# A mixture-of-experts layer in two waves: batches split five to three, denser dispatch in attention, a shorter gather at the end

## The chip, the cores and the metric

The kernel runs on one core of one Trainium2 chip. The metric is the device time of one execution in microseconds. The program is written by hand for the engines: PE (TensorE, matrix products), ACT (ScalarE), DVE (VectorE), POOL (GpSimd) and SP (SyncE, which here only issues DMA transfers). Each engine works through its own list of instructions in order; they meet only in semaphores.

## The reference

Input x is 8 batches of 512 tokens of 256 float32 values. What is computed:

```
q = elu(x@Wq+bq)+1;  k = elu(x@Wk+bk)+1;  v = x@Wv+bv        # 16 heads of 16
kv   = einsum('bhsd,bhse->bhde', k, v)                        # per batch
attn = einsum('bhsd,bhde->bhse', q, kv)
x = layernorm(x + (sigmoid(x@Wg+bg) * attn) @ Wo + bo)
# routing: softmax over 16 experts in 4 groups, the best 2 groups, the best 4 experts in them
y = sum over the 4 chosen experts e of  c[t,e] * (silu(x@w1[e]) * (x@w3[e])) @ w2[e]
z = (silu(x@ws1) * (x@ws3)) @ ws2                             # shared expert
x = layernorm(x + y + z)
```

There are 4096 tokens and so 16384 pairs of token and expert. Experts have an inner width of 128, the shared one of 256.

## The kernel before

**Layout.** Batch b has 4 tiles of 128 tokens; tile k is tile k % 4 of batch k // 4. All activations stay on the chip in `x_all`.

**Attention and routing (to about 270 us).** PE, DVE and POOL have `batch` (PE from L1228, DVE from L902) written out eight times. For batch b the engines project, sum k and v, attend to batch b, and finish batch b-1: residual and layer norm (DVE `bn_stats` L691 and `bn_aggr` L699, then POOL `rstd_of` L424 to L431 with four small operations, then ACT L510), transposes of the result, `route` (PE L1211/L1212, whose products DVE reads at L730) and, for batch b-2, `assign_slots` (DVE L793 to L804), which gives each token its four rows in a table sorted by expert.

**Dispatch.** POOL's `dispatch` (L434 to L441) writes 128 token rows of 1 KB into this table in DRAM (`expert_in`) with one indirect DMA: one per tile and choice, so 16 per batch. The table has a part for each of two waves of four batches, and 64 dispatches fill one. In each of the attention batches b = 3 to 7 POOL has four places for `SPREAD` = 3 of them: after `kv_projected`, after `rstd_of(b-1)` (these two and the third come close together), after `q_projected`, and after `kv_summed`. The last 4 follow. The 64 of wave 1 are sent in sixteen bursts of four while PE works on wave 0, the i-th gated by the pair 5i//2.

**Planning.** When batch 3's slots are known, `count_region` (called in batch 5) tells SP where regions end, and `plan_pairs` cuts the table into pairs of 256 rows: 48 per wave. The instructions L844, L849, L850 and L854 go over 48x16 numbers on one partition.

**Experts.** A pair is one block of 256 rows: SP loads it, PE transposes (L1340), multiplies up (L1149 to L1151) and down (L1367), ACT does silu (L634) and copies, DVE the product (L1036) and the low parts (L1025, L1044), SP stores the result into `expert_out`. The ring has four places; PE, ACT and SP run in hardware loops, DVE too in most of each wave. The shared expert runs for three batches (`EARLY`) ahead of the pairs and for five after them.

**Gathering.** POOL's `gather` (L443 to L454) fetches, for one tile, four times 128 rows from `expert_out`, into one of four places `y_got`; DVE's `combine` (L1055) adds each, weighted, to `x_all`. All 16 tiles of wave 0 are gathered and combined while the pairs of wave 1 run, at one or two combines per pair, with final norms of batches 0 to 2. The gather of tile k waits for `combined` of tile k-4.

**The end.** After the last store of `expert_out`, POOL gathers wave 1's 16 tiles: four batches of 16 indirect DMAs, with `rstd_of(NB + b - 1)` after the gathers of batch b. Meanwhile PE and ACT do the shared expert of batches 3 to 7, and DVE takes, in a fixed order, `shared_hidden`, 8 of the tiles' combines inside it, `add_shared(n)` (L1002), the final norm (L1070) and the moments (L691, L699); the other 8 tiles come after `add_shared(7)`. SP stores each batch's output of 512 KB when its norm is done.

## Time and profile before

| what | value |
|---|---|
| median of three runs | 701.73 us (698.48 to 703.09) |
| the profiled execution | 698.33 us, its span 696.5 us |
| mean granted clock of TensorE | 0.925 |
| attention and routing | 0 to about 270 us |
| wave 0's pairs | about 270 to 437 us |
| wave 1's pairs, to the last store | about 437 to 590 us |
| gathers of wave 1, remaining sums and norms | 590 to 696.5 us |

The profile is of one execution on the only core. "Idle before" an instruction is given in brackets with what ended it; `remote` or `another core or an unknown queue` stands where the profile finds no releaser in its records (there is no other core at work here). `issue` is time in which an engine waited for nothing that the profile shows. Where ACT or DVE work in a pair, the names of tiles are those of buffers used again (`kv_heads` is silu's result, `q_fm`, `gate` and `wa_stage` hold gathered rows, `gated` the output).

### The profile page before, as it was taken

The numbers are of one execution on the slowest core, as the hardware profiler recorded it, in microseconds if no ns is written. First come the engines' busy times: TensorE is split into PE (matmuls) and PEld (weight loads), VectorE is DVE, ScalarE is ACT, GpSimd is POOL, SyncE is SP. The second block draws the span as 40 slices with busy tenths as digits, with TensorE's granted clock in tenths as the row PEclk, the third lists the DMA queues.
The fourth block names the chain that finished last, engine by engine and source line by source line (L and its number), as shares of the span: only waits on it lengthen the run. The fifth ranks groups of instructions, "written<-read, shape, count | busy, mean of one in ns | idle before, by whom it ended". The sixth has DMA issues, their size and how long they took to land.

```text
span 696.5 us, 13485 instructions
## 1 busy us (share of the span) xinstructions
PE 517.0 (74%) x3554; PEld 355.2 (51%) x3555; DVE 427.1 (61%) x1200; ACT 300.6 (43%) x659; POOL 290.6 (42%) x334
## 2 busy tenths in 40 slices
PE   1899886789897787888886787888887779782300
PEld 1355543455454356676674566676765666441100
DVE  2447783777755877557654344366757657585384
ACT  2536644446334252555554555355645446121000
POOL 1000126365455421545644200634435450787664
PEclk9999999799999989999999999899999999997555
DMA  7022338285561302677767776677777763334232
GB/s 193 25 76 77 124 118 288 75 274 192 202 225 54 113 31 69 220 231 241 252 243 247 252 226 210 189 232 226 222 246 230 240 198 137 99 120 123 83 113 98
DMA packets 64091, 118.63 MB, mean 170 GB/s; under 512 B 9760, under 2 KB 23088, under 8 KB 64048
## 3 DMA queue, kind: packets, MB, share of 16 engines
q1 hardware_dynamic: 51216, 84.55, 37.2%
q0 software_dynamic: 12288, 33.57, 15.4%
q8 instruction: 19, 0.31, 0.2%
q14 instruction: 24, 0.20, 0.1%
q10 hardware_dynamic: 544, 0.00, 0.0%
HBM read 55.17 MB, written 62.91 MB: 170 GB/s over the span
## 4 chain that ended last, share of the span: by engine, by line
PE 35%; issue 17%; DVE 17%; SPq 8%; POOL 7%; ACT 5%; DMA 5%; another core or an unknown queue 5%; DVEq 0%; ACTq 0%; POOLq 0%
PE t L1340 4%; PE h_even L1149 3%; PE h_even L1151 3%; PE h_even L1150 3%; PE h_odd L1149 3%; PE h_odd L1151 3%; PE h_odd L1150 3%; DMA kv<-expert_in 2%; PE y L1186 2%; SPq L327 2%; POOL q_fm L452 2%; SPq L330 2%; POOL wa_stage L452 2%; POOL gate L452 2%
## 5 line engine op out<-in xcount | busy, mean ns | idle before, releaser
L440 POOL DMA_INDIRECT expert_in<-x_all,slots x128 | 132.9, 1038 | 111.7 <-PE h_odd L1151 45.1
L1340 PE MATMUL t<-ident,kv 128*128 128x128 f32 x384 | 61.7, 283 | 23.8 <-DMA kv<-expert_in 16.6
L452 POOL DMA_INDIRECT wa_stage<-expert_out,result_of x64 | 62.9, 982 | 28.2 <-issue 17.5
L452 POOL DMA_INDIRECT q_fm<-expert_out,result_of x32 | 32.1, 1003 | 89.8 <-DMA expert_out<-q_exp 64.1
L1044 DVE TENSOR_TENSOR wa_lo<-bias_heads,wa_hi 128x256 bf16<-128x256 f32 x96 | 40.5, 422 | 46.6 <-ACT wa_hi L642 37.2
L426 POOL TENSOR_SCALAR neg_mean<-mv 128x4 f32<-128x4 f32 x16 | 4.6, 290 | 148.7 <-DVE mv L699 148.5
L1340 PEld LDWEIGHTS t<-ident,kv 128*128 128x128 f32 x384 | 44.9, 145 | 33.8 <-issue 17.6
L1025 DVE TENSOR_TENSOR xsT_lo<-t,xsT_hi 128x512 bf16<-128x512 f32 x72 | 49.4, 688 | 13.2 <-ACT xsT_hi L617 6.6
L1150 PE MATMUL h_even<-xsT_lo,we_hi 128*128 128x256 bf16 x192 | 53.6, 279 | 2.2 <-issue 2.2
L1149 PE MATMUL h_even<-xsT_hi,we_hi 128*128 128x256 f16 x192 | 53.5, 279 | 1.8 <-DVE bias_heads L1036 1.3
L1151 PE MATMUL h_even<-xsT_hi,we_lo 128*128 128x256 f16 x192 | 53.6, 279 | 1.2 <-issue 1.1
L617 ACT ACTIVATE xsT_hi<-t 128x512 f16<-128x512 f32 x72 | 42.1, 587 | 17.9 <-PE t L1340 12.7
L1367 PE MATMUL y<-we_hi,wa_hi 128*128 x96 | 26.9, 281 | 27.8 <-issue 15.5
L642 ACT ACTIVATE wa_hi<-bias_heads 128x256 f16<-128x256 f32 x96 | 39.7, 413 | 16.0 <-DVE bias_heads L1036 10.6
L1186 PE MATMUL y<-wo_sb,gated 128*128 128x256 f32 x128 | 33.5, 421 | 12.0 <-DVE gated L686 12.0
L452 POOL DMA_INDIRECT gate<-expert_out,result_of x32 | 31.2, 976 | 19.7 <-PE h_even L1151 10.8
L1036 DVE TENSOR_TENSOR bias_heads<-h_odd,kv_heads 128x256 f32<-128x256 f32 x48 | 20.1, 420 | 31.4 <-ACT kv_heads L634 31.4
L1036 DVE TENSOR_TENSOR bias_heads<-h_even,kv_heads 128x256 f32<-128x256 f32 x48 | 20.1, 419 | 31.3 <-ACT kv_heads L634 19.2
L624 ACT ACTIVATE q_exp<-y 128x512 f32<-128x512 f32 x48 | 28.6, 597 | 23.4 <-PE y L1373 18.1
L529 ACT ACTIVATE kv<-h_even 128x256 f32<-128x256 f32 x32 | 12.4, 386 | 59.4 <-PE h_even L1151 53.1
L1186 PEld LDWEIGHTS y<-wo_sb,gated 128*128 128x128 f32 x128 | 26.8, 213 | 19.2 <-DVE gated L686 14.7
L634 ACT ACTIVATE kv_heads<-h_odd 128x256 f32<-128x256 f32 x48 | 18.3, 382 | 41.9 <-remote 22.0
(222 smaller groups left out, 1522.0 us busy)
## 6 DMA issues: line engine op xcount, KB each, us to landing
kv<-expert_in SPq DMA_DIRECT2D x96, 256.0 KB
expert_out<-k_exp SPq DMA_DIRECT2D x48, 256.0 KB
expert_out<-q_exp SPq DMA_DIRECT2D x48, 256.0 KB
expert_in<-wa_stage SPq DMA_DIRECT2D x16, 512.0 KB
expert_in<-wa_stage SPq DMA_DIRECT2D x32, 256.0 KB
stage<-in_L_ffn_w SPq DMA_DIRECT2D x48, 128.0 KB
x_in<-in_L_attn_x SPq DMA_DIRECT2D x8, 512.0 KB
out<-gated SPq DMA_DIRECT2D x8, 512.0 KB
```

The source lines that it names most:

```text
L440: pool.indirect_dma_start(xs_dram[b // WB], bass.IndirectOffsetOnAxis(ap=slots[:, b, t, j:j + 1], axis=0), x_all[:, b, t, :], None).then_i ...
L452: pool.indirect_dma_start(y_got[i][:, j, :], None, ys_dram[w], bass.IndirectOffsetOnAxis(ap=result_of[:, b, t, j:j + 1], axis=0)).then_inc ...
L617: act.activation(xsT_hi[r][:, :, :], t_bank[r % 2][:, :].rearrange("p (c n) -> p c n", c=KC), ACT.Copy).then_inc(xst_hi_ready, 1)
L642: act.activation(aT_hi[r % 2][:, :], a_pair, ACT.Copy).then_inc(at_hi_ready, 1)
L1025: dve.tensor_tensor(xsT_lo[r][:, :, :], t_bank[r % 2][:, :].rearrange("p (c n) -> p c n", c=KC), xsT_hi[r][:, :, :], ALU.subtract).then_in ...
L1036: dve.tensor_tensor(a_pair, h_banks[r % 2][0][:, 2 * P:], s_pair, ALU.mult).then_inc(pair_a_ready, 1)
L1044: dve.tensor_tensor(aT_lo[r % 2][:, :], a_pair, aT_hi[r % 2][:, :], ALU.subtract).then_inc(at_lo_ready, 1)
L1149: pe.matmul(dst, sta_hi, mov_hi, start=start, stop=False)
L1150: pe.matmul(dst, sta_hi, mov_lo, start=False, stop=False)
L1151: return pe.matmul(dst, sta_lo, mov_hi, start=False, stop=stop)
L1186: last = pe.matmul(y_bank[h][:, (t % 2) * D:(t % 2 + 1) * D], gated[:, c, t * P:(t + 1) * P], wo_sb[:, c, :], start=c == 0, stop=c == KC - 1)
L1340: last = pe.transpose(t_bank[r % 2][:, c * 2 * P + i * P:c * 2 * P + (i + 1) * P], xs[r][:, i, c * P:(c + 1) * P], ident[:, :])
```

## The change

The waves get five and three batches, so 56 and 40 pairs instead of 48 and 48. In the attention stage all 80 dispatches of wave 0 are sent, 16 in each of the batches 3 to 7 (`SPREAD` 4) and none after; the 48 of wave 1 follow in twelve bursts of four, one every four pairs of wave 0. `count_region(0)` moves from batch 5 to batch 6. The planning operations of both waves are made for up to 56 pairs.

In wave 1, DVE's code is written out pair by pair. It combines 18 of wave 0's 20 tiles (72 combines) evenly over the pairs 6 to 39, and the final norms of batches 0 to 2 lie one tile per pair at pairs 16, 23 and 31. POOL's gathers of these 20 tiles are gated at pair 17k//9 of wave 1.

At the end 12 tiles are gathered instead of 16. Ten tiles (18 to 27) are combined inside the shared expert's steps, four (batch 7) after `add_shared(7)`. The final `rstd` is made of two POOL operations instead of four, and their places between the gathers change. The last batch has moments, `rstd`, norm and output store in two halves; the `rstd` of its first half is asked for ahead of the gather of its last tile.

```diff
-SPREAD = 3
+SPREAD = 4
@@
-    WB = NB // WAVES
-    WT = WB * TT
-    NPAIR = WT * TOP_K // 2 + E
+    BATCHES = (5, 3)
+    START = (0, BATCHES[0], NB)
+    TILES = [TT * n for n in BATCHES]
+    NPAIR = [n * TOP_K // 2 + E for n in TILES]
+    SUM_PAIRS = (6, 40)
+    SUMMED = 18
+    NORM_PAIR = (16, 23, 31)
@@ sync
-            with sp.Fori(WB - 2, NB) as b:
+            with sp.Fori(EARLY - 1, NB - 1) as b:
                 store_out(b)
-            sp.wait_ge(out_stored, 16 * NB)
+            for h in range(2):
+                half = slice(2 * h, 2 * h + 2)
+                sp.wait_ge(out_ready, NB + h)
+                sp.dma_start(out[NB - 1].rearrange("(p t) d -> p t d", p=P)[:, half, :], o_sb[:, half, :]).then_inc(out_stored, 16)
+            sp.wait_ge(out_stored, 16 * (NB + 1))
@@ gpsimd
+            def final_rstd(ln, of=slice(0, TT)):
+                pool.wait_ge(mv_ready, ln + 1)
+                pool.tensor_tensor(var_eps[:, of], mv[:, of, 1], eps[:, of], ALU.add).then_inc(rstd_step, 1)
+                pool.wait_ge(rstd_step, NB + ln + 1)
+                pool.tensor_tensor(rstd[:, of], var_eps[:, of], minus_half[:, of], ALU.pow).then_inc(rstd_ready, 1)
@@ gather(k)
-                if 0 < k < WT:
-                    pool.wait_ge(h_ready, NPAIR + (3 * k if k < WT - TT else 3 * WT - 13 + 2 * (k - WT + TT)))
+                if w == 0 and k > 0:
+                    pool.wait_ge(h_ready, FIRST[1] + 17 * k // 9)
@@
-            for i in range(WT):
+            for i in range(TILES[1]):
                 if i > 0:
-                    pool.wait_ge(h_ready, 5 * i // 2)
+                    pool.wait_ge(h_ready, 4 * i)
                 dispatch(rows[first + TOP_K * i:first + TOP_K * (i + 1)])
@@
                         gather(TT * b + t)
-                        if b > 0 and t == (1 if w == 0 else TT - 1):
-                            rstd_of(NB + b - 1)
-            rstd_of(2 * NB - 1)
+                        if w == 0 and t == TT - 2 and 0 < b <= EARLY:
+                            final_rstd(NB + b - 1)
+                        if b == NB - 1 and t == 1:
+                            final_rstd(2 * NB - 2)
+                        if b == NB - 1 and t == 2:
+                            final_rstd(2 * NB - 1, slice(0, 2))
+                    if w == 1 and b < NB - 1:
+                        for ln in range(EARLY if b == START[1] else b - 1, b):
+                            final_rstd(NB + ln)
+            final_rstd(2 * NB, slice(2, TT))
@@ vector
-            batch(5, True, True, True, early=PAIRS - 1, plan=True)
-            batch(6, True, True, True)
+            batch(5, True, True, True, early=PAIRS - 1)
+            batch(6, True, True, True, plan=True)
@@
-            with dve.Fori(1, EARLY) as b:
-                group(q1 + 1 + 3 * b, b, thirds[0])
-                group(q1 + 2 + 3 * b, b, thirds[1], norm=b - 1)
-                group(q1 + 3 + 3 * b, b, thirds[2])
+            for i in range(SUMMED * TOP_K):
+                at = SUM_PAIRS[0] + i * (SUM_PAIRS[1] - SUM_PAIRS[0]) // (SUMMED * TOP_K)
+                sums[at].append((i // (TT * TOP_K), i // TOP_K % TT, i % TOP_K))
+            for p in range(NPAIR[1]):
+                pair(FIRST[1] + p, p % RING, p < NPAIR[1] - 2, sums[p], norms.get(p))
@@
-            for n in range(WB, NB):
-                at = 2 * (n - WB)
+            for n in range(EARLY, NB):
+                at = SHARED * (n - EARLY)
                 shared_hidden(SHARED * n, tiles[at])
                 shared_hidden(SHARED * n + 1, tiles[at + 1])
@@
-            for b in range(WB + 2, NB):
-                for t in range(TT):
-                    for j in range(TOP_K):
-                        combine(1, b, t, j)
-                    if t == 2:
-                        whole_norm(b - 1)
-            whole_norm(NB - 1)
+            for w, b, t in tiles[SHARED * (NB - EARLY):]:
+                for j in range(TOP_K):
+                    if (t, j) == (1, TOP_K - 1):
+                        whole_norm(b - 1)
+                    combine(w, b, t, j)
+                if t >= 2:
+                    final_norm(b, 2 * t - 4)
+                    final_norm(b, 2 * t - 3)
```

## Rows read from the trace of the kernel before

**Rows 1.** The page: span, busy time and instructions of the engines.
```profile
span 696.5 us, 13485 instructions
PE 517.0 (74%) x3554; PEld 355.2 (51%) x3555; DVE 427.1 (61%) x1200; ACT 300.6 (43%) x659; POOL 290.6 (42%) x334
```

**Rows 2.** The last chain, 100 to 240 us: start, length, what.
```profile
110.49 10.35 another core or an unknown queue
...
145.49 3.38 another core or an unknown queue
...
173.17 3.31 another core or an unknown queue
```

**Rows 3.** Timeline of POOL, dispatches and a wait beside attention: start, us, what [idle before].
```profile
102.87 2.00 POOL L440 DMA_INDIRECT expert_in<-x_all,slots  x1 [0.18 <-issue]
...
118.02 0.96 POOL L440 DMA_INDIRECT expert_in<-x_all,slots  x1 [0.30 <-issue]
...
148.29 0.96 POOL L440 DMA_INDIRECT expert_in<-x_all,slots  x1 [0.30 <-issue]
...
175.98 0.96 POOL L440 DMA_INDIRECT expert_in<-x_all,slots  x1 [0.30 <-issue]
...
187.52 0.23 POOL L426 TENSOR_SCALAR neg_mean<-mv 128x4 f32<-128x4 f32 x1 [5.06 <-DVE mv L699]
```

**Rows 4.** Timeline of DVE, where it takes the router's products, and a planning operation.
```profile
86.61 0.29 DVE L730 TENSOR_REDUCE logits<-t 128x64 f32<-128x128 f32 x1 [0.81 <-PE t L1212]
...
120.85 0.29 DVE L730 TENSOR_REDUCE logits<-t 128x64 f32<-128x128 f32 x1 [10.37 <-remote]
...
227.81 0.29 DVE L730 TENSOR_REDUCE logits<-t 128x64 f32<-128x128 f32 x1 [1.95 <-remote]
...
232.53 0.94 DVE L844 TENSOR_TENSOR stage<-plan_sb,pairs_end 1x768 f32<-1x768 f32 x1
```

**Rows 5.** Timeline of PE: the router's last product of batch 2.
```profile
111.07 0.18 PE L1212 MATMUL t<-gwT_both,xT_lo 128*128 128x32 f16 x1
```

**Rows 6.** Timeline of ACT, one silu per pair: pairs 2, 51, 52, 59, 91, 95.
```profile
277.55 0.38 ACT L634 ACTIVATE kv_heads<-h_even 128x256 f32<-128x256 f32 x1
...
436.83 0.38 ACT L634 ACTIVATE kv_heads<-h_odd 128x256 f32<-128x256 f32 x1 [0.28 <-PE h_odd L1151]
446.22 0.38 ACT L634 ACTIVATE kv_heads<-h_even 128x256 f32<-128x256 f32 x1 [6.58 <-remote]
...
466.06 0.38 ACT L634 ACTIVATE kv_heads<-h_odd 128x256 f32<-128x256 f32 x1 [0.28 <-PE h_odd L1151]
...
574.56 0.38 ACT L634 ACTIVATE kv_heads<-h_odd 128x256 f32<-128x256 f32 x1 [0.94 <-remote]
...
582.81 0.38 ACT L634 ACTIVATE kv_heads<-h_odd 128x256 f32<-128x256 f32 x1 [0.41 <-PE h_odd L1151]
```

**Rows 7.** Timeline of POOL: gathers at the start of wave 1.
```profile
436.18 1.21 POOL L452 DMA_INDIRECT q_fm<-expert_out,result_of  x1 [46.19 <-DMA expert_out<-q_exp]
...
445.20 0.95 POOL L452 DMA_INDIRECT gate<-expert_out,result_of  x1 [0.30 <-issue]
```

**Rows 8.** Timeline of POOL: the end.
```profile
590.97 0.94 POOL L452 DMA_INDIRECT q_fm<-expert_out,result_of  x1 [17.95 <-DMA expert_out<-q_exp]
...
611.80 0.26 POOL L426 TENSOR_SCALAR neg_mean<-mv 128x4 f32<-128x4 f32 x1
...
663.71 1.07 POOL L452 DMA_INDIRECT q_fm<-expert_out,result_of  x1 [4.82 <-DVE x_all L1055]
...
690.12 0.23 POOL L426 TENSOR_SCALAR neg_mean<-mv 128x4 f32<-128x4 f32 x1 [4.34 <-DVE mv L699]
```

**Rows 9.** Timeline of DVE: the end.
```profile
652.84 1.29 DVE L1002 TENSOR_TENSOR x_all<-y,x_all 128x512 f32<-128x512 f32 x2 [7.88 <-remote]
...
680.76 2.05 DVE L1055 SCALAR_TENSOR_TENSOR x_all<-wa_stage,c_of_slot,x_all 128x256 f32<-128x256 f32 x4 [2.57 <-DMA wa_stage<-expert_out,result_of]
...
691.94 1.38 DVE L1070 TENSOR_SCALAR gated<-x_all,mv,rstd 128x256 f32<-128x256 f32 x4 [1.91 <-POOL shift L431]
```

More of the change, by code:

```diff
@@ L353, in _ @@
             sp.wait_ge(rows_ready, 1)
-            for b in range(WB):
+            for b in range(BATCHES[0]):
                 sp.wait_ge(dispatched[b], 16 * TT * TOP_K)
@@ L364, in _ @@
             sp.wait_ge(fill_rows_ready, 2)
-            with sp.Fori(3, (last - 1) // 2) as q2:
+            with sp.Fori(3, 5) as q2:
                 group(0, 2 * q2 + 1, fill=E + 2 * RING * (q2 - 3))
                 group(0, 2 * q2 + 2, fill=E + 2 * RING * (q2 - 3) + RING)
+            for q in range(11, last):
+                group(0, q)
             sp.wait_ge(rows_ready, 2)
-            for b in range(WB, NB):
+            for b in range(BATCHES[0], NB):
                 sp.wait_ge(dispatched[b], 16 * TT * TOP_K)
@@ L693, in norm_stats, with norm_moments @@
                 norm_moments(ln)
-            def norm_moments(ln):
+            def norm_moments(ln, of=slice(0, TT)):
                 dve.wait_ge(bn_ready, ln + 1)
                 dve.memset(wait_pad[:, :], 0.0)
-                for t in range(TT):
+                for t in range(TT)[of]:
                     last = dve.bn_aggr(mv[:, t, :], bn[:, t, :])
@@ L868, in place_results @@
                     tiles = slot_of[:, of_wave, :, :].rearrange("p b t e -> p (b t) e")
-                    dve.tensor_tensor(tiles, tiles, closer[:, w:w + 1, :].to_broadcast([P, WT, E]), ALU.add).then_inc(result_step, 1)
+                    dve.tensor_tensor(tiles, tiles, closer[:, w:w + 1, :].to_broadcast([P, TILES[w], E]), ALU.add).then_inc(result_step, 1)
                 if part in (1, 2):
                     dve.wait_ge(result_step, at + 1)
-                    for b in range(WB * w + 2 * part - 2, WB * w + 2 * part):
+                    middle = START[w] + (BATCHES[w] + 1) // 2
+                    for b in range(*((START[w], middle) if part == 1 else (middle, START[w + 1]))):
                         for t in range(TT):
@@ L939, in batch @@
                 if plan:
-                    count_region(0, WB - 1)
+                    count_region(0, BATCHES[0] - 1)
             xt_lo(0)
@@ L1026, in xst_lo, with pair @@
                                   xsT_hi[r][:, :, :], ALU.subtract).then_inc(xst_lo_ready, 1)
-            def pair(g, r, ahead=True, add=None, norm=None, whole=True, part=None):
+            def pair(g, r, ahead=True, add=(), norm=None, part=None):
                 if ahead:
@@ L1044, in pair, with combine @@
                 dve.tensor_tensor(aT_lo[r % 2][:, :], a_pair, aT_hi[r % 2][:, :], ALU.subtract).then_inc(at_lo_ready, 1)
-                if add and len(add) > 1:
-                    combine(0, *add[1], whole)
-            def combine(w, b, t, j, whole=True):
+                for some in add[1:]:
+                    combine(0, *some)
+            def combine(w, b, t, j):
                 if j == 0:
                     dve.wait_ge(y_gathered[t], 16 * TOP_K * (b + 1))
-                if late(b, 1) or t > 0 or j > 0:
+                if b > 0 or t > 0 or j > 0:
                     dve.wait_ge(combined, TOP_K * (TT * b + t) + j)
@@ L1060, in combine @@
                     last = dve.bn_stats(bn[:, t, :], x_all[:, b, t, :])
-                    if t == TT - 1:
+                    if b == NB - 1 and t % 2 == 1:
+                        last.then_inc(bn_ready, 1)
+                        norm_moments(2 * NB - 1 + t // 2, slice(t - 1, t + 1))
+                    elif t == TT - 1:
                         last.then_inc(bn_ready, 1)
@@ L1065, in final_norm @@
             def final_norm(b, t):
+                halved = b == NB - 1
+                if halved and t == 2:
+                    dve.wait_ge(rstd_ready, 2 * NB + 1)
                 if t == 0:
@@ L1071, in final_norm, with group @@
                                          ALU.subtract, ALU.mult)
-                if t == TT - 1:
+                if t == TT - 1 or (halved and t == 1):
                     last.then_inc(out_ready, 1)
-            def group(q, b=None, tiles=(), norm=None, whole=True, parts=(), last=False):
+            def group(q, parts=()):
                 for r in range(RING):
-                    add = [(b, i // TOP_K, i % TOP_K) for i in tiles[r]] if tiles else None
-                    pair(RING * q + r, r, not (last and r >= 2), add, norm, whole,
-                         parts[r] if r < len(parts) else None)
-            q1 = GROUPS_OF_PAIRS
+                    pair(RING * q + r, r, part=parts[r] if r < len(parts) else None)
+            q1 = PAIR_GROUPS[0]
             xst_lo(0, 0)
```

128 lines of the change are left out of this document (62 added, 66 removed).

## The prediction

> **What bounds the kernel now.** I read the page first. PE is busy for 517 of 696.5 us, DVE for 427, POOL for 291 [rows 1]; no engine fills the span, so the stages have different limits and each is read by itself.
>
> *Attention.* The chain of waits that ended last, between 100 and 240 us, shows three long pieces with no releaser in the records: 10.35, 3.38 and 3.31 us [rows 2]. The reader should ask who was late. The router's last product for batch 2 is issued at 111.07 and takes 0.18 us [rows 5]. Yet DVE takes the result only at 120.85, after 10.37 us of idling; in the batch before, with no dispatch beside it, the same step waited 0.81 us [rows 4]. POOL's timeline fits: a burst of 12 dispatches from 102.87 to 118.98, and the bursts of batches 4 and 5 end at 149.25 and 176.94 [rows 3], within half a microsecond of the ends of the other two pieces, 148.87 and 176.48. So while POOL issues indirect DMAs back to back, the news that PE's product is done reaches DVE late. I call it a hold. What carries it no view shows.
>
> *Pairs.* One silu on ACT per pair is the clock: pairs 2 to 51 take 159.3 us (3.25 each), pairs 59 to 95 take 116.75 (3.24 each) [rows 6]. Where two tiles are gathered back to back, from 436.18 to 446.15 [rows 7], the next silu comes at 446.22, 9.39 us after the one before [rows 6]: a hold again. After the second such place the last four pairs run in 8.25 us, 2.06 each, from 574.56 to 582.81 [rows 6], with two combines each. So DVE with two combines keeps up at 2.1 us per pair, and about 1.2 us per pair is waiting that a hold makes or that is caught up behind it.
>
> *End.* Gathers start at 590.97, when the last result has landed; 16 tiles in four batches, `rstd_of` after each. The first 16 DMAs go from 590.97 to 611.80, 1.3 us each; the last batch's 16 start at 663.71 after a wait of 4.82 for DVE [rows 8]. The last combines are 2.05 us a tile; then moments, POOL's `rstd` at 690.12, norm 691.94 to 693.32 [rows 8, 9], and the store to 696.5. POOL sets the end, apart from that wait, whose cause is `add_shared` of batch 6, 7.88 us late at 652.84 [rows 9] for PE's products of the shared expert (a hold too, by its `remote`).
>
> **The change part by part,** against the profiled execution's span of 696.5 us (its time, 698.33, is 1.8 more).
>
> *Dispatch beside attention.* Four more indirect DMAs per batch. One costs 0.96 and a gap of 0.3: 1.26 us (12 in 16.1 us with a first one of 2.0 [rows 3]). The burst of batch 3 becomes 16 long, +5.0; those of 4 and 5, 9 long now, become 12, +3.8 each. The trace puts the hold's end at the burst's end, and the holds are on the chain, so this goes through one to one: 12.6. In batches 6 and 7 the burst is broken by POOL's waits, and the router's result of batch 6 comes 1.95 us late in the middle of a burst [rows 4]: anything from 0 to +8 for the two, I take +2. Against it: work behind the hold can close up, and the four left-over dispatches after batch 7 go. Value +12, ends 0 (holds do not grow) and +20. POOL's `rstd` of the next batch, queued behind the longer burst, idled 5.06 us for its moments [rows 3], which four dispatches more (5.0) just fill: nothing, but if moments came earlier it would be late by up to that.
>
> *Planning.* Four chained operations of 0.94 us at 768 elements [rows 4] grow to 896, 0.13 each: +0.5 in wave 0, between attention and the first load. `count_region` one batch later makes SP's end fills start some 26 us later, near 205; the first pair's load came at 237, so 30 us cover them: nothing. If that cover went, its 16 small stores would be in front of the loads.
>
> *Pairs.* There are still 96. Wave 0 gets 8 more and 12 bursts of four instead of 16, and its pace with the bursts in it, 3.25, is that of later pairs, 3.24: 0. Wave 1 has 40 pairs, and 18 tiles' combines (72 for 34 pairs, 2.1 per pair instead of 1.33) with 20 tiles' gathers in them: one gather of 5.0 us per 1.9 pairs. If each holds the pairs for its 5.0 us and the pairs catch up at 2.06 (0.9 of them), a tile costs 6.9 us, 3.6 us per pair: 36 x (3.6 - 3.24) = +13. The first three tiles of gathers are due at once, a burst of 12 instead of 8, of which +5 is within this. But wave 1 of before also had the 9.39 us place twice and this one has it once: -3. Value +10, ends 0 (3.24 holds) and +20. The new output stores of batches 0 and 1 in SP's list wait for norms at pairs 19 and 26; loads queued behind them are four pairs ahead: nothing.
>
> DVE's code in wave 1 is written out where it ran in a loop. No row here separates the two: The 3.24 was measured with the loop. The Trainium skill ("Runtime: NRT & Kernel Launch", Instruction fetch mechanics) says that a taken branch breaks the sequential prefetch and that full unrolling is preferred for it; by it this is a gain, of a size that no row gives, and the sum leaves it at nothing.
>
> *End.* With T = 590.97 for the last store: gathers of tiles 20 to 23 are issued by 611.5 (5.1 a tile), `rstd` of batch 3 by 613.4, then batch 4's moments are awaited: DVE reaches them behind `add_shared(4)` at 620.7 by the step lengths of before. `rstd` is then 1.5 us instead of some 1.9 (four operations, 690.12 to 691.94 [rows 8, 9]). Tiles 24 to 27 go to 642.6, `rstd` 644.1, tiles 28 and 29 to 654.4, `rstd` 655.9, tile 30 to 661.0, the first half's `rstd` at 663.8 (it waits for the moments of tiles 28 and 29), tile 31 to 669, landing 671.2, combines 673.3, moments 674.2, `rstd` 675.7, half a norm 676.5, a half store 679.4. That is 17 us earlier. It supposes that the shared expert's last sums come when due. If they come as late as before, at 652.84 for batch 6 [rows 9] and so near 660 for batch 7, the steps after it are the sum 1.3, tiles 28 and 29 with a norm 6.4, the half `rstd` 1.5, behind it the gather of tile 31 5.1 and 2.2 to land, its combines 2.05, and 6.1 for moments, `rstd`, half norm and half store: 684.7, a gain of 12; with the 7.88 us of lateness once more, 4. Value -12, ends -17 and -4. Two `rstd` operations less are 0.4 us per batch on POOL, the last one on the chain; the halves save about 0.7 of norm and 0.6 of moments at the very end; both are in it.
>
> *Sum:* 12 + 0.5 + 10 - 12 = +10.5: span 707, time 708.8. The profiled execution lies 3.4 below the median of the runs shown; from the median it would be 712. I take **710.0**.
>
> **Rivals.**
>
> 1. *Holds do not grow (the other side).* If what ends a hold is one event near the burst's end (a result that would have been late anyway), or if lengthening is taken up by slack of later engines, terms one and three fall to near nothing and the end's gain of 12 to 17 stands alone: 701.7 - 12 = 690, or 686. For it: batch 6's result came in the middle of a burst, 1.95 us late [rows 4], and in pairs a burst of four costs nothing in the mean pace. Against it: three burst ends in a row within half a microsecond to two of the release. It decides from where the two hold terms together are under 5 us. Chance 0.33.
>
> A rule speaks for it. The Trainium skill ("SBUF — State Buffer", SBUF: two separate sides) has engine and DMA ports disjoint: a compute engine and a DMA cannot slow each other, and only POOL's writing of descriptors can starve. By it a burst of DMAs could not hold PE's results at all. The 10.37 us beside the 0.81 disagree with that or have another cause; with another cause the time would be this rival's, 690.
>
> 2. *One of the two places takes it up.* Attention grows by 12 but wave 1 keeps 3.24 per pair, or the reverse: sum 0 to +2, time 699 to 704. Chance 0.24.
>
> 3. *DVE becomes the bound in wave 1.* 0.8 combines more per pair, at 0.51 us each (four in 2.05 [rows 9]), every one on the path, are 0.4 us x 36 = +14: instead of the hold term time 714, on top of it 724. Against it the 2.06 us pairs with two combines. Chance 0.1.
>
> 4. *My forecast,* both holds grow and the end shortens: 706 to 714 by itself. Chance 0.33.
>
> **How the numbers follow.** Faster or slower means by over 1%, about what a measurement of this kernel can tell from no change: under 694.7 or over 708.7. Rival 1 gives faster 0.3, same 0.03; rival 2 same, with a little on both sides; rival 3 slower; my forecast slower 0.28 and same 0.05. Together faster 0.33, same 0.26, slower 0.41. The range for 8 in 10 reaches from the end of rival 1, 686, to 721, the upper ends of one of the hold terms.
>
> **What would show each step.** In attention: DVE's waits for the router's products, near 15 us in batch 3 and 7 in batches 4 and 5, and the first pair's silu near 286 instead of 274 (rival 1: 274 to 276). In the pairs: the silu of wave 1's pairs 3.5 us apart, with waits of 3 us on `remote` at each tile's gather; for rival 3 the waits would be ACT's on DVE. At the end: from the first gather to the end of the span 93 us instead of 105.5. What would make me wrong most: that a hold is a property of PE's instruction stream at that place and not of POOL's burst, so that its length has nothing to do with `SPREAD`.

## The result: slower by 4.5 per cent, and the profile after

| | before | after |
|---|---|---|
| median | 702.08 us | 733.3 us (730.15 to 736.54, four runs) |
| ratio, with its 95% interval | | 1.0455 (1.0394 to 1.0515) |
| profiled execution, span | 696.5 | 734.8 |
| first silu of the pairs (end of attention) | 273.9 | 296.3 |
| first to last silu (96 pairs) | 308.9 | 341.8 |
| last silu to the end | 113.7 | 96.7 |

The three parts differ by +22.4, +32.9 and -17.0 us, together the 38.3 of the two spans (the profiled execution after is the slowest of its four; the medians are 31 apart). The prediction had +12.5, +10 and -12.

The page of the kernel after: PE's busy time grows from 517 [rows 1] to 543 us for the same 3554 matmuls, and the mean granted clock is 0.886 where it was 0.925, with more sevens and eights in attention and in the last third.

```profile
span 734.8 us, 13362 instructions
PE 542.6 (74%) x3554; PEld 370.5 (50%) x3555; DVE 425.6 (58%) x1197; ACT 301.4 (41%) x659; POOL 286.2 (39%) x320
...
PEclk9999997889988789999999999987987988899765
```

*Attention.* DVE's waits for the router's products, the rows that answer to [rows 4] (start, us, what, idle before):

```profile
124.69 0.29 DVE L755 TENSOR_REDUCE logits<-t 128x64 f32<-128x128 f32 x1 [13.89 <-remote]
...
153.74 0.29 DVE L755 TENSOR_REDUCE logits<-t 128x64 f32<-128x128 f32 x1 [4.84 <-remote]
...
182.13 0.29 DVE L755 TENSOR_REDUCE logits<-t 128x64 f32<-128x128 f32 x1 [3.35 <-remote]
...
216.87 0.29 DVE L755 TENSOR_REDUCE logits<-t 128x64 f32<-128x128 f32 x1 [7.99 <-remote]
...
249.64 0.29 DVE L755 TENSOR_REDUCE logits<-t 128x64 f32<-128x128 f32 x1 [9.05 <-remote]
```

The holds of POOL batches 3, 4 and 5 grew by 3.5, 1.4 and 0.0 us; those of batches 6 and 7, 2.00 and 1.95 before, are 7.99 and 9.05. POOL's timeline shows why these two: in batch 6 the dispatches are now one unbroken burst of twelve, where POOL's waits had cut it into six, three and three (batch 7 likewise has twelve in a row, where it had six and seven).

```profile
199.81 1.86 POOL L458 DMA_INDIRECT expert_in<-x_all,slots  x1 [0.17 <-issue]
...
214.89 0.96 POOL L458 DMA_INDIRECT expert_in<-x_all,slots  x1 [0.30 <-issue]
```

*Wave 1.* POOL's gathers open with a burst of 16 (four tiles), from 478.96 to 498.9; the gates of tiles 0 to 3 (pairs 0, 1, 3 and 5) had all passed. ACT's timeline, three silus in a row, beside [rows 6]:

```profile
478.57 0.39 ACT L659 ACTIVATE kv_heads<-h_odd 128x256 f32<-128x256 f32 x1 [0.28 <-PE h_odd L1179]
...
483.25 0.38 ACT L659 ACTIVATE kv_heads<-h_even 128x256 f32<-128x256 f32 x1 [2.64 <-remote]
...
501.68 0.38 ACT L659 ACTIVATE kv_heads<-h_odd 128x256 f32<-128x256 f32 x1 [10.66 <-remote]
```

One pair took 18.4 us. PE's timeline has the last matmul of the product that this silu reads, and it is not late:

```profile
483.07 0.27 PE L1179 MATMUL h_odd<-xsT_hi,we_lo 128*128 128x256 f16 x1
```

Where no burst runs, a silu starts 0.04 us after its product ends; this one starts 18.3 us after, 2.8 us past the end of the burst. The trace's record of the semaphore says the same: PE's update for this product stands at 501.66. (The profile models when a matmul ends; when it starts and when a semaphore is updated are records.) So the hold is a late message, as the prediction had it. Measured in this way (start of the reader less end of the product's last matmul) the five holds of attention are 13.8, 4.8, 3.3, 7.2 and 9.8 us, before 9.6, 3.3, 3.2, 2.9 and 1.6, and 47 of the 96 silus come over 1 us late, before 57. A burst of four is enough: beside the one from 386.1 to 390.9 the silu is 3.4 us late.

```profile
388.17 0.27 PE L1179 MATMUL h_even<-xsT_hi,we_lo 128*128 128x256 f16 x1
```
```profile
391.85 0.38 ACT L659 ACTIVATE kv_heads<-h_even 128x256 f32<-128x256 f32 x1 [3.55 <-remote]
```

PE's own pace falls too, behind that product. In the windows of PE (us, PE busy and number of matmuls, granted clock, share of the DMA engines, GB/s) it does 39 matmuls in 4 us, and then 4, 3, 2 and 5:

```profile
480.00:484.00 4.00, 4.00 (x39) 1.00 0.79 254
486.00:490.00 4.00, 1.03 (x4) 0.83 0.57 174
490.00:494.00 4.00, 1.11 (x3) 0.50 0.60 180
494.00:498.00 4.00, 0.74 (x2) 0.50 0.34 98
498.00:502.00 4.00, 1.34 (x5) 0.50 0.23 66
```

and its timeline shows matmuls of the next pair, with no wait between them in the program, issued 0.7 or 1.4 us apart. The releaser is `issue`: PE waited for nobody.

```profile
488.98 0.37 PE L1178 MATMUL h_even<-xsT_lo,we_hi 128*128 128x256 bf16 x1 [1.15 <-issue]
490.39 0.37 PE L1179 MATMUL h_even<-xsT_hi,we_lo 128*128 128x256 f16 x1 [1.04 <-issue]
491.09 0.37 PE L1177 MATMUL h_even<-xsT_hi,we_hi 128*128 128x256 f16 x1 [0.33 <-issue]
```

So two things happen beside a burst: the news of PE's products is late, and in a long burst PE itself crawls. The combines, which DVE does pair by pair, come late with them, POOL gets behind its gates (it waits for `combined`) and then sends two tiles at once: two places of eight gathers in a row before, five after. The mean of wave 1's pairs 56 to 95 is 4.31 us.

*End.* From the first gather after the last store to the end of the span: 645.5 to 734.8, 89.3 us, where it was 590.97 to 696.5, 105.5 [rows 8].

### The profile page after: what moved, and what is told of

It reads as the page before. It is cut to its first block, busy times and chain, and to the rows that moved or that the text cites. A ratio compares the mean times of both kernels' runs of the same rounds, so it can differ in the third digit from the quotient of the medians.

```text
span 734.8 us, 13362 instructions
## 1 busy us (share of the span) xinstructions
PE 542.6 (74%) x3554; PEld 370.5 (50%) x3555; DVE 425.6 (58%) x1197; ACT 301.4 (41%) x659; POOL 286.2 (39%) x320
## 4 chain that ended last, share of the span: by engine, by line
PE 35%; DVE 19%; another core or an unknown queue 14%; issue 12%; ACT 7%; SPq 5%; POOL 4%; DMA 4%; ACTq 0%; POOLq 0%; DVEq 0%
PE t L1368 4%; PE h_even L1177 3%; PE h_even L1179 3%; PE h_even L1178 3%; PE y L1214 3%; PE h_odd L1179 3%; PE h_odd L1177 3%; DVE x_all L1085 3%; PE h_odd L1178 2%; DMA kv<-expert_in 2%; DVE bn L716 2%; ACT x_all L535 1%; PE y L1395 1%; PE t L1184 1%
## 5 line engine op out<-in xcount | busy, mean ns | idle before, releaser
L458 POOL DMA_INDIRECT expert_in<-x_all,slots x128 | 130.8, 1022 | 157.7 <-PE h_odd L1179 112.6
L1368 PE MATMUL t<-ident,kv 128*128 128x128 f32 x384 | 64.3, 291 | 18.8 <-DMA kv<-expert_in 12.3
L470 POOL DMA_INDIRECT wa_stage<-expert_out,result_of x64 | 62.7, 980 | 32.2 <-issue 18.3
L1178 PE MATMUL h_even<-xsT_lo,we_hi 128*128 128x256 bf16 x192 | 55.9, 291 | 7.8 <-issue 7.8
L1177 PE MATMUL h_even<-xsT_hi,we_hi 128*128 128x256 f16 x192 | 55.6, 290 | 8.0 <-issue 5.3
L1368 PEld LDWEIGHTS t<-ident,kv 128*128 128x128 f32 x384 | 48.1, 150 | 26.4 <-issue 12.9
L1179 PE MATMUL h_even<-xsT_hi,we_lo 128*128 128x256 f16 x192 | 55.8, 290 | 5.6 <-issue 5.5
L1214 PE MATMUL y<-wo_sb,gated 128*128 128x256 f32 x128 | 38.8, 470 | 23.5 <-DVE gated L711 22.4
L437 POOL TENSOR_SCALAR neg_mean<-mv 128x4 f32<-128x4 f32 x8 | 1.8, 228 | 128.6 <-DVE mv L724 128.6
L659 ACT ACTIVATE kv_heads<-h_even 128x256 f32<-128x256 f32 x48 | 18.3, 382 | 73.1 <-remote 39.6
L1214 PEld LDWEIGHTS y<-wo_sb,gated 128*128 128x128 f32 x128 | 30.5, 243 | 32.3 <-DVE gated L711 24.8
L1395 PE MATMUL y<-we_hi,wa_hi 128*128 x96 | 27.6, 288 | 22.8 <-issue 14.6
```

What stands on the lines that cost most here:

```text
L458: pool.indirect_dma_start(xs_dram[0 if b < BATCHES[0] else 1], bass.IndirectOffsetOnAxis(ap=slots[:, b, t, j:j + 1], axis=0), x_all[:, b, ...
L470: pool.indirect_dma_start(y_got[i][:, j, :], None, ys_dram[w], bass.IndirectOffsetOnAxis(ap=result_of[:, b, t, j:j + 1], axis=0)).then_inc ...
L1177: pe.matmul(dst, sta_hi, mov_hi, start=start, stop=False)
L1178: pe.matmul(dst, sta_hi, mov_lo, start=False, stop=False)
L1179: return pe.matmul(dst, sta_lo, mov_hi, start=False, stop=stop)
L1214: last = pe.matmul(y_bank[h][:, (t % 2) * D:(t % 2 + 1) * D], gated[:, c, t * P:(t + 1) * P], wo_sb[:, c, :], start=c == 0, stop=c == KC - 1)
```

## The experiments

Theory A: a long burst of indirect DMAs on POOL starves the other engines of instructions. ("Starve" is my word here for independent instructions issued far apart; that instructions are what is lacking is a reading of that pattern, and no view shows their supply.) B: the data they move does. C, D, E: the kernel's own waits, DVE as bound of wave 1, POOL's whole busy time. Each series ran beside the kernel before on the same chip; ratios are to that.

**micro1: bursts beside nothing but matmuls.** PE: 2200 matmuls written out, then loops; POOL (shortened), each at a given point of PE's progress:

```
for at, what, n in PLAN: ...          # gathers of 128 rows of 1 KB: 4, 8, 16; 16 with a pause
    pool.indirect_dma_start(got[:, j, :], None, xf, IndirectOffsetOnAxis(ap=index[:, j:j+1], axis=0))
    if what == "spaced" and j % 2 == 1: pool.memset(fill[:, :], 0.0)      # 0.97 us
```

> Leaves the whole computation out: PE runs matmuls of 128x256 fp16 back to back, 2200 of them written out, then in a loop with a body of 25, then in a loop with a body of 400, while POOL sends bursts of 4, 8 and 16 indirect gathers, 16 gathers with a pause of a memset after every second, 8 plain DMAs, and 12 memsets; the output is x of batch 0. Theory A (a burst of indirect DMAs starves PE of instructions): PE keeps 0.11 us per matmul for some 50 matmuls (100 instructions) after a burst begins, then steps at 0.7 us per instruction to the burst's end; so the 16-burst (20 us) costs PE over 10 us of progress, the 4-burst (4.7 us) near none, the one with pauses clearly less than the 16-burst, memsets nothing; the loop with a body of 25 matmuls, that needs no new instructions, is not slowed. Theory B (data traffic of the gathers, or SBUF writes): slowed alike in all three forms of code, plain DMAs too. Theory C (the holds come from the kernel's own waits): no slowing anywhere.

Measured, windows of PE. The burst of 16 lasts from 85.6 to 105.3, the spaced one from 144.3 to 169.8, the one beside the loop with a body of 25 from 297.2 to 316.9:

```profile
84.00:86.00 2.00, 2.00 (x21) 1.00 0.00 0
92.00:94.00 2.00, 2.00 (x19) 1.00 0.41 127
94.00:96.00 2.00, 0.80 (x5) 1.00 0.29 78
100.00:102.00 2.00, 0.59 (x2) 0.55 0.33 100
108.00:110.00 2.00, 1.64 (x8) 0.50 0.00 0
156.00:158.00 2.00, 2.00 (x21) 1.00 0.41 123
168.00:170.00 2.00, 2.00 (x21) 1.00 0.22 66
304.00:306.00 2.00, 1.98 (x19) 1.00 0.33 105
308.00:310.00 2.00, 0.38 (x4) 1.00 0.25 78
```

For some 8 us, six or seven DMAs, PE keeps its pace: 21 matmuls are at work within each 2 us, and 9.2 start per us. Then it falls to five and fewer, until one to three us past the burst. The burst of 4 costs this stream nothing, that of 8 its last two us, and the 16 with a pause after every second nothing at all. Theory C falls. The stream waits for nobody, though, so it can't show what late news costs; but POOL is told PE's progress by a semaphore, and the update of the matmul issued at 304.80 stands at 319.91, past the burst, where outside bursts it comes with the matmul's end. The loop with a small body starves like the written-out code, so my guess that it would be spared was wrong, and nothing here depends on code being new to PE. The granted clock is still 2.4 GHz (1.00) in the window in which PE has fallen to five matmuls, and 1.2 (0.50) only behind it: it follows.

**after_gates: the gathers' gates later, nothing else.**

```diff
-                    pool.wait_ge(h_ready, FIRST[1] + 17 * k // 9)
+                    pool.wait_ge(h_ready, FIRST[1] + 3 + 36 * k // 19)
```

> The kernel after, with one edit: the gathers of wave 0's tiles are gated at pair 3 + 36k/19 of wave 1 instead of 17k/9, so that the first four tiles are not gathered in one burst of 16 indirect DMAs. Theory A: the 18 us of hold at the start of wave 1 (silu of pair 60 to that of pair 61) shrinks to about 3, later bursts of 8 split; wave 1 gains 8 to 18 us, time about 718. Theory D (DVE, with 2.1 combines per pair, is the bound of wave 1): no gain, or a loss of some us since tiles come later: 733 to 738.

1.0006 (0.9973 to 1.0039), 708.95 against 709.26 us. The opening burst is 8 long instead of 16, the rest go by fours; pairs 56 to 95 take 131.9 us instead of 168.2, a gain of 36 where I expected 8 to 18. By the ratios (1.0455 and 1.0006, on different chips) this one line gives back the whole net loss. D falls: the same combines, and 3.4 us per pair instead of 4.3.

**after_plain: wave 0's tiles by plain DMAs.** `gather` issues one `pool.dma_start` of 512 KB per tile, of fixed rows, so that the sums are not the right ones.

> The kernel after, but in wave 1 each of wave 0's 20 tiles is fetched by one plain POOL DMA of 512 KB with fixed rows instead of four indirect ones; the sums so made are of the wrong rows. Same bytes, same combines on DVE, one descriptor job instead of four. Theory A: wave 1 at 3.0 to 3.3 us per pair instead of 4.3, time 733 - 35 = 698 or so. Theory B (the traffic itself): no change of more than 5 us. Theory D (DVE's combines): no change.

0.9801 (0.9746 to 0.9856), 694.41 us; pairs 56 to 95 in 111.9 us, 2.87 each. With the same bytes by plain DMAs no silu of wave 1 is over 1 us late behind its product, where after_gates has 34; against B. It also prices the 8 and the fours that are left in after_gates: 20 us. Fours are not free.

**before_spread4: the attention edit alone, in the kernel before.** `SPREAD = 4`, so 16 dispatches beside batches 3 to 6, none later.

> The kernel before with the attention edit alone: 16 dispatches beside each of the batches 3 to 6, none beside 7 and none after (before: 12 beside each of 3 to 7, then 4). Waves, gathers and the end are as before. Theory A (a burst may be 6 to 8 indirect DMAs long before PE slows, everything beyond adds one to one): the hold of batch 3 goes from 10.4 to 14 or 15 us, those of 4 and 5 from 3.4 to 4 or 5, batch 6 from 2 to 8; batch 7 has none: the first pair's silu comes 8 to 14 us later than in before, time + 8 to + 14. If attention's share of the loss came from elsewhere (count_region one batch later, planning): no change, within 2 us.

1.0211 (1.0174 to 1.0248): + 14.6 us, the first silu at 287.9 instead of 273.9. The holds are 14.6, 4.9, 4.9 and 9.1; again batch 6, with its new burst of 12, pays most (batch 7, now without dispatches, waits 0.81).

**before_paused and after_paused: the bursts cut by pauses.** The pause is a POOL operation of the kernel's own kind:

```diff
+            def pause():
+                if pauses[0]:
+                    pool.wait_ge(paused, pauses[0])
+                pool.tensor_tensor(pause_pad[:, :], eps[:, :], minus_half[:, :], ALU.pow).then_inc(paused, 1)
+                pauses[0] += 1
@@ between the dispatches beside attention, and in gather:
+                pause()
                 for j in range(TOP_K):
```

> The kernel before with a pause of one POOL operation of 1.04 us on four numbers after every third dispatch beside attention and ahead of every tile's four gathers. Theory A: no more than three or four indirect DMAs are back to back, so PE is fed: DVE's waits for the router's products fall to 1 us in batches 3 to 7, the two places with a hold of 6 to 9 us in wave 1 go, PE is not slow at the end; POOL's own end path grows by 16 pauses of 1.3 us = 21 us where it was the bound, less what DVE gains. Attention gains 15 to 20 us, the waves 5 to 10, the end loses 10 to 20: total -5 to -20. Theory E (POOL's whole busy time, not unbroken bursts, decides): attention no better, total +10 to +30.

> The kernel after with the later gates (pair 3 + 36k/19) and with the same pauses: after every fourth dispatch beside attention and ahead of every tile's four gathers. Theory A: attention as fast as without bursts or nearly (first silu at 270 instead of 299), unless POOL, now 20 + 4 us busy per batch of 26, is late itself; wave 1 near 3.0 us per pair; 12 pauses of 1.3 us at the end; total 20 to 35 us under after_gates. Theory E: no gain.

before_paused 0.9867 (0.9821 to 0.9913), after_paused (with the later gates) 0.9839 (0.9801 to 0.9876). Attention ends at 265.2 and 277.1. DVE's waits in batches 3 to 7 are 1.31, 0.62, 2.74, 2.94 and 0.81 us in before_paused, where batch 3 had 10.37 [rows 4]; the two near 3 are still held, so runs of three with a pause are not clean either. Attention gained 8.7 us against the trace of before where I expected 15 to 20, and after_paused is some 12 us under after_gates by the ratios, not 20 to 35. E falls: POOL does more and the engines do better. The end pays: last silu to the end 125.7 and 107.7 us, where POOL is the bound and a pause is time.

**micro2: how long a pause, and who starves.**

> Leaves the whole computation out, as micro1: 3400 matmuls written out on PE, POOL sends 16 gathers with a pause after every fourth of 1.0 us, 0.5 us, and 0.1 us, 15 with 0.5 us after every third, 16 with a wait for landing after every fourth, 12 with 1.0 us after every sixth, and 16 without pause, the last one while DVE and ACT run streams of small operations. Theory A: a pause of 1.0 us after every fourth leaves PE at 10.5 matmuls per us; 0.1 us does not help (the gap between two DMAs is 0.3 already) and PE falls to 2 per us after some 8 us; 0.5 us lies between. DVE and ACT: if the shortage is one of instructions for all engines, their streams step at 0.7 us per operation too from some 8 us into the burst; if it is PE's own, they go on at their pace.

Matmuls started in the last 8 us of 16 gathers (74 is full): with 0.1 us after every fourth 9, 0.5 us 20, 1.0 us 31 (full until 14 us into it; I had expected it to be full throughout). The 15 with 0.5 us after every third have 26, the 12 with 1.0 us after every sixth 30. With a wait for landing after every fourth the pace is full throughout, and that series of 16 took 24.9 us instead of 19.7. With DVE and ACT working too (their streams, no waits in them):

```profile
358.88 0.42 DVE L61 TENSOR_REDUCE d_out<-x_sb 128x1 f32<-128x256 f32 x1 [0.98 <-issue]
359.60 0.42 DVE L61 TENSOR_REDUCE d_out<-x_sb 128x1 f32<-128x256 f32 x1 [0.29 <-issue]
361.01 0.42 DVE L61 TENSOR_REDUCE d_out<-x_sb 128x1 f32<-128x256 f32 x1 [1.00 <-issue]
```
```profile
353.25 0.21 ACT L68 ACTIVATE s_out<-x_sb 128x4 f32<-128x4 f32 x1 [1.13 <-issue]
353.97 0.20 ACT L68 ACTIVATE s_out<-x_sb 128x4 f32<-128x4 f32 x1 [0.51 <-issue]
355.38 0.20 ACT L68 ACTIVATE s_out<-x_sb 128x4 f32<-128x4 f32 x1 [1.21 <-issue]
```

Both step at 0.7 and 1.4 us, and PE starts 4 matmuls in the last 8 us, where it started 9 in the series with 0.1 us: the shortage is common to all. It does not begin for all at once. All 400 operations of each stream are in the trace: ACT, at one operation per 0.1 us, has its first gap 3.6 us into the burst, PE 5.8, and DVE, at one per 0.33 us, only after 15. Counted in what each had started since the burst began it is 38 operations, 53 matmuls and 47 operations, nearer to each other than the times; alone, in micro1, PE had started 76.

**before_tail: the edits of the end alone.** The final rstd in two operations, the last batch in halves, in the kernel before.

> The kernel before with the last two edits alone: the final rstd in two POOL operations, and moments, rstd, norm and store of the last batch in two halves (its rstd of the first half ahead of the gather of its last tile). By the terms of the prediction: 0.4 us per rstd on POOL in four places, 0.7 of norm and 0.6 of moments on the last chain, a half store instead of a whole one: -2 to -4 us. If the end is set by PE's late sums of the shared expert instead: -1 us, within the noise.

0.9925 (0.9897 to 0.9954), 4 us. But the kernel before took 644.48 us here, not 702 to 710, and that was the surprise of the study.

**before_best: before_paused, no pauses ahead of the last six tiles, with the edits of the end.**

> Before_paused with the same two edits of the end, and without pauses ahead of the gathers of the last six tiles, when PE's work is nearly done: before_paused's 0.987 of before, less 6 pauses of 1.3 us and less 2 to 3 us of the edits: 0.970 to 0.978, 689 to 694 us where before is 709.7. If the longer bursts of the last six tiles hold PE's last sums again, only the edits' 2 to 3 us: 0.983.

1.011 (1.0077 to 1.0144) in the same series: the pauses cost and gave nothing. For there, a burst did not starve PE:

**micro3** (the same chip).

> Leaves the whole computation out: 3000 matmuls written out on PE; POOL sends 32 plain DMAs of 128 KB back to back, then 16 indirect gathers of 64 rows instead of 128, then 16 of 128 rows, each with its own semaphore on which DVE takes the time of landing; then SP sends 8 plain loads of 512 KB through the hardware's queue. If the shortage is one of DMA traffic by bytes: the plain DMAs (128 KB in 0.55 us, twice the bytes per us) and SP's loads slow PE more than the gathers. If it comes from POOL making descriptors for indirect rows, or from the rows themselves piling up in the DMA queues: plain DMAs do nothing or little, the 64-row gathers slow PE less or later, and for piling up the landing of the k-th gather lags its issue by more and more (2 us at first, 5 or more at the last); with a constant lag of some 2 us nothing piles up in the queues and the making of descriptors is left.

The last two us of 16 gathers in a row, 168 to 170, in PE's windows:

```profile
162.00:164.00 2.00, 2.00 (x21) 1.00 0.37 113
168.00:170.00 2.00, 2.00 (x21) 1.00 0.46 131
```

POOL issues at the same pace (0.95 us and a gap of 0.30), the landings are about as prompt (2.7 us for most, 3.8 at most), PE goes on, and its updates come with its matmuls. Whether a burst starves the engines depends on the chip. Of the five chips of these series two are of this kind (before 644 us), three of the first (before 701 to 710 us); the result above, before at 702, has the first kind's holds.

**after_again, micro3_again: once more, on a chip of the first kind.**

> The kernel after, unchanged, once more beside before. In the last series the kernel before took 644.5 us instead of 702 to 710, and a burst of 16 indirect gathers left PE at its pace (21 matmuls in each 2 us to its end): whether a burst starves the engines depends on the chip. Theory A: on a chip where bursts starve, the ratio is 1.045 again, attention + 22 to 25 us, wave 1 + 30; on one where they do not, the hold terms vanish, the end's 12 to 17 us stay, and the ratio is 0.975 to 0.995. If the loss has another cause than starved engines: 1.03 to 1.05 on either.

> The same as micro3, to be read on this chip. Where a burst of 16 gathers of 128 rows slows PE: if by bytes, the 32 plain DMAs in 17 us slow it more; if by the making of descriptors or by piled-up rows, they do not, and the 64-row gathers slow it less or later; piled-up rows show in landings that lag their issue by more and more. On a chip without starving: 21 matmuls in each 2 us all through.

after_again 1.0456 (1.0351 to 1.0562), its three parts 296.2, 334.3 and 94.8 us. In micro3_again the windows are of 32 plain DMAs, then twice of 16 gathers of 64 rows (94.9 to 113.9), of 16 of 128 rows (163.9 to 183.7), and of SP's loads:

```profile
46.00:48.00 2.00, 2.00 (x21) 1.00 0.75 246
...
102.90:104.90 2.00, 1.21 (x12) 1.00 0.11 33
106.90:108.90 2.00, 0.49 (x3) 0.89 0.23 66
...
175.90:177.90 2.00, 0.75 (x3) 0.70 0.32 100
...
275.00:277.00 2.00, 2.00 (x21) 1.00 0.93 379
```

246 and 379 GB/s of other traffic do nothing; gathers at 33 to 66 GB/s starve. Half the rows starve as soon as all of them. DVE's marks for the first and the last landing, beside POOL's issues:

```profile
166.76 0.15 DVE L62 COPY d_out<-x_sb 128x1 f32<-128x1 f32 x1 [161.85 <-DMA got<-in_L_attn_x,index]
...
185.57 0.15 DVE L62 COPY d_out<-x_sb 128x1 f32<-128x1 f32 x1 [1.20 <-DMA got<-in_L_attn_x,index]
```
```profile
163.94 0.97 POOL L81 DMA_INDIRECT got<-in_L_attn_x,index  x1 [50.02 <-PE h L112]
...
182.76 0.94 POOL L81 DMA_INDIRECT got<-in_L_attn_x,index  x1 [0.30 <-issue]
```

2.8 us both: nothing piles up. B is out. What is left, by exclusion and not by a view that shows it, is POOL's own work on an indirect DMA, without a rest of a microsecond or two, on some chips.

**after_best, after_third: the other kind again.** after_best has the later gates and pauses beside attention only.

> The kernel after with the later gates (pair 3 + 36k/19) and pauses of 1.04 us in its dispatches beside attention only (in after_paused the pauses ahead of the gathers brought wave 1 nothing, 135.1 us for pairs 56 to 95 against 131.9, and cost the end 8 us). Theory A, on a chip where bursts starve the engines: after_gates' 1.0006 less the 22 us that attention gained in after_paused: 0.965 to 0.975. On a chip where they do not: between 0.97 and 0.99, the end's gain alone. If attention's 22 us were a difference of chips: 1.0.

> The kernel after, unchanged, beside before on this chip. Theory A: where bursts starve the engines 1.045 again; where they do not 0.975 to 0.995. If the loss is one of order and waits that any chip shows: 1.03 or more on either.

Before 644.28 us. **The change itself is 0.9826 (0.978 to 0.9872) here, 633.95 us:** faster. after_best 0.9929 (0.9896 to 0.9961). In the profile of after_third DVE's waits for the router are those of a batch without dispatches, though POOL sends 16 and more in a row beside them, and even 28 in a row in wave 1; all eight of the router's products are read 0.04 us after their end, and no silu of the 96 is over 0.14 us late:

```profile
144.68 0.29 DVE L755 TENSOR_REDUCE logits<-t 128x64 f32<-128x128 f32 x1 [0.76 <-PE t L1240]
...
222.79 0.29 DVE L755 TENSOR_REDUCE logits<-t 128x64 f32<-128x128 f32 x1 [0.81 <-PE t L1240]
```

Its three parts are 269.5, 267.8 and 95.3 us; those of before_tail, the nearest profile of that kind, 265.2, 269.4 and 106.4.

**after_best_again, before_best_again: the first kind.**

> The same as after_best: later gates, pauses beside attention only. Theory A, where bursts starve (before near 700 to 710): 0.965 to 0.975, first silu near 277 instead of 296 to 299, wave 1 near 3.4 us per pair. If attention's gain in after_paused came from elsewhere: 1.0.

> The same as before_best, wanted on a chip where bursts starve: pauses beside attention and ahead of the gathers of the first 26 tiles, and the two edits of the end. Theory A, there: before_paused's 0.987 less some 10 us = 0.970 to 0.978. On the other kind 1.01 again.

after_best 0.9717 (0.9689 to 0.9745), 686.98 against 707.08 us; before_best 0.9782 (0.9743 to 0.9821). So after_best beats both kernels where bursts starve, before by 2.8 per cent and the change by 5.5 (medians on the same chip, 727.0 against 687.0) to 7 (ratios); on the other kind it beats before by 0.7, and the unmended change is a per cent ahead of it. The best of both, gates late and no pauses, was not run there.

## Why the prediction was wrong, point by point

**What bounds the kernel.** The rows and their reading held. That holds exist, where, and that POOL's bursts make them, is shown by before_paused and micro1. "The news that PE's product is done reaches DVE late" holds as well: 9.6 us behind the product in batch 3 before, 0.04 in every batch of after_third. What carries it no run shows. Three things the reading did not have: in long bursts the engines' own pace falls too; a burst of four already makes the news up to 3.6 us late; and "the trace puts the hold's end at the burst's end" is not general, for after the change the holds of batches 4 and 5 end 2.7 and 4.2 us ahead of it.

**Dispatch beside attention,** the first step that failed: +12 forecast, +22.4 measured. The mechanism was right, the sizes were not. I priced batches 3 to 5 at one to one (12.6) and batches 6 and 7 at +2. Measured from the changes of the five waits: 5.0 for the first three and 13.1 for the last two; the other 4 us lie in smaller waits that I did not trace one by one. In batch 3 four dispatches more added 3.5 us, near their length of 5.0; in batches 4 and 5 the hold ended before the burst did, and why stays open. In batches 6 and 7 the router's product now comes 9.6 and 8.1 us into an unbroken burst of twelve and is held until 1.0 and 2.1 us past its end: I had read the late result in a broken burst as a sign of small holds, and did not ask what `SPREAD` 4 does to the breaks. "Anything from 0 to +8 for the two" was the bound that broke. On the other kind of chip, where nothing is held, attention still grows by 4.3 us (269.5 in after_third, 265.2 in before_tail): there POOL's `rstd` of batch 3 starts at 129.57, straight behind a burst of twenty, instead of 126.63, the lateness that the prediction named as possible. On the first kind POOL still idles 4.4 to 5.2 us ahead of the `rstd` of batches 3 to 6.

**Pairs,** the second and larger: +10 forecast, ends 0 and 20; +32.9 measured (+25.4 in after_again, against the same trace of before). The price of a tile that is gathered by itself was about right: with the later gates pairs 56 to 95 take 3.4 us each, and the step "a tile costs 6.9 us" gave 3.6. What failed is the step after it, "the first three tiles of gathers are due at once, a burst of 12 instead of 8, of which +5 is within this". It was 16, and the pairs 60 to 64 took 25.0 us instead of 10.3. And I left out the loop that follows: news comes late, the combines come late, POOL waits for `combined`, is behind its gates and sends eights. after_gates, which removes only this, gives it back. Fours have their price too, in both kernels: 47 pairs of wave 0 took 150.5 us before, with fifteen of them, and after, with eleven, but 136.7 (before_tail) and 133.6 (after_third) on the other kind of chip.

**Planning and wave 0** came as forecast: the four planning operations take 1.07 us instead of 0.94, wave 0's 47 pairs the same time. **DVE as bound,** rival 3, fell with after_gates. That written-out code on DVE would help, by the Trainium skill's rule on taken branches ("Runtime: NRT & Kernel Launch", Instruction fetch mechanics), no run here shows: pairs 56 to 95 take 2.83 us each in after_third, written out, and 2.73 in the loop of before_tail, but the first has 2.1 combines per pair and the second 1.33, so the two do not separate it.

**End,** right in kind, small in size: -12 forecast with -17 as its end; from the first gather to the end of the span, as the prediction counted, -16.2 measured (-17.0 from the last silu), near the undisturbed schedule of the prediction. The two edits of the last batch and of rstd are worth 4 us of it on the other kind (before_tail); I had some 3.

**The rivals.** Rival 1, holds that do not count, 690 or -12 us, is what happens on the other kind of chip: -10.3 us. I gave it 0.33 and asked whether holds grow; the question was on which chip. The rule named beside it (the Trainium skill, "SBUF — State Buffer", SBUF: two separate sides: compute and DMA cannot slow each other) holds for the traffic, as 379 GB/s with 21 matmuls shows (micro3_again), and says nothing of PE's signals or of the pace at which engines issue, which is where the time went. On the chip of the record my own forecast, both holds grow and the end shortens, was the right one of the four in kind, with the hold terms at half and a third of their size (12 for 22.4, 10 for 32.9). The range ended at 721 because it took only one of the two at its upper end, +20, and both went past that.

## What to carry to other kernels

When an engine's wait has no releaser in the records, look at the timeline of the engine that should have released it before putting a price on the wait. If the product was issued long before and the engine went on at its pace, the message is late; if instructions with no wait between them are issued 0.7 us apart, the engine crawls. Here both happened, and the first made the holds. Keep indirect DMAs on POOL to runs of four or so with a wait or an operation of its own between them while others compute (even those cost some us here), gate them by the consumer's progress late enough that they can't bunch, and leave the pauses out where POOL is the bound. When a change makes bursts denser, ask which breaks in them it removes. And measure on more than one chip: this change is 4.5% slower on one kind and 1.7% faster on the other.

## What the runs showed of the hardware that I had not expected

- On three of five chips here, PE's semaphore updates come late beside indirect DMAs issued back to back on POOL (1.25 us each): up to 3.6 us in a burst of four, 18.3 us in one of sixteen, and soon after the burst. The updates of DVE, ACT and POOL that could be matched to their instructions in the traces of before and after are never over 0.02 us late.
- On the same chips the engines' own pace falls in a long burst. PE alone falls after some 8 us, from 9.2 matmuls per us to about 1, and to 0.5 when ACT and DVE run too; there ACT falls first, after 3.6 us, and the slower stream of DVE after 15. A wait for landing after every fourth, or 1 us of other POOL work after every second, avoids it; 0.1 us after every fourth does not.
- It goes by POOL's time in a burst, not by rows or bytes: 64 rows starve like 128, plain DMAs at 246 GB/s and hardware queues at 379 GB/s not at all, and landing stays at 2.8 us.
- On two chips it did not happen, and the same kernel took 644 us instead of 701 to 710. What differs between the chips, and whether one cause is behind the late updates and the slow issue, stays open. The transfers of instructions are not it, as far as the traces show: the page has 43 packets of the instruction queues in both kinds of run; in micro1 the one of 16 KB that starts inside the burst of 16, at 88.4, takes 0.98 us, those outside 0.89 to 1.33; and none is recorded from 257 to 369, the time of the loop with a body of 25, in which PE starved all the same.
- The granted clock went to 1.2 GHz behind each long starving, so the first us after a burst are slower still: in micro1 12 matmuls per 2 us from 110 to 114, where 21 is full.
